# Who issues the second filter's two loads of a head: SyncE or ScalarE

## The reference, cut to what matters

```python
# 64 heads, head_dim 8; k = v = context, q = layernorm(x)
kv = einsum('bhil,bhjl->bijhl', k, v)
y = irfft(rfft(kv, 2L) * rfft(ssm_kernel, 2L))[..., :L]      # causal convolution along l, one filter per head
out = y + kv * D
x = x + tanh(g0) * einsum('bijhl,bhil->bjhl', out, q)
x = x + tanh(g1) * mixture_of_experts(layernorm(x))          # one shared expert, 7 routed, top 2, capacity 1170
```

## Time and profile before

| | |
|---|---|
| median of 3 runs | 4374.21 us (4369.9 to 4388.32) |
| profiled execution | 4357.41 us, span 4355.6 us |
| TensorE busy | 4130.0 us, 95% |
| VectorE, ScalarE, GpSimd busy | 60%, 44%, 23% |
| queue of SyncE (q1, hardware) | 413.89 MB, 31.6% of 16 DMA engines |
| queue of GpSimd (q0, software) | 218.41 MB, 26.7% |

### The profile page before, as it was taken

The page is one execution under the profiler, slowest core; times in us unless marked ns, Lnnn a source line. Parts: engine busy times, 40 slices in busy tenths (PEclk is TensorE's granted clock), DMA queues, the critical chain, the costliest instruction groups (busy, mean ns, idle before and its releaser), DMA issues.

```text
span 4355.6 us, 71272 instructions
## 1 busy us (share of the span) xinstructions
PE 4130.0 (95%) x25930; PEld 3766.7 (86%) x25930; DVE 2608.2 (60%) x2980; ACT 1898.5 (44%) x2451; POOL 997.7 (23%) x1200
## 2 busy tenths in 40 slices
PE   6999999999999999996899999999999999999997
PEld 6899999999999999996688888888888988988986
DVE  6899999999999999996434441222323332333331
ACT  6777777777777777774211111111112211121120
POOL 1232322232322332331000014451001211211111
PEclk9999999999999999998899999999999999999999
DMA  7878888878888888886532333423433443344332
GB/s 167 207 192 217 204 220 198 214 196 218 198 217 196 217 197 213 198 218 160 72 116 72 102 89 106 116 83 93 120 108 97 92 102 97 82 111 97 78 96 49
DMA packets 280375, 634.14 MB, mean 146 GB/s; under 512 B 45840, under 2 KB 111866, under 8 KB 280246
## 3 DMA queue, kind: packets, MB, share of 16 engines
q1 hardware_dynamic: 218582, 413.89, 31.6%
q0 software_dynamic: 61664, 218.41, 26.7%
HBM read 311.03 MB, written 170.16 MB: 110 GB/s over the span
## 4 chain that ended last, share of the span: by engine, by line
PE 48%; DMA 2%; DVE 1%; issue 1%; ACT 0%; SPq 0%; POOL 0%; DVEq 0%; POOLq 0%; ACTq 0%
PE moe_ps L1644 11%; PE moe_ps L1645 11%; PE moe_ps L1646 11%; PE moe_ps L1662 5%; PE moe_ps L1663 5%; PE moe_ps L1664 5%; PE moe_psT L1633 1%; DMA out<-moe_y,moe_add_i 1%; DVE moe_zl L1542 1%; DMA moe_y<-out 0%; ACT moe_zh L1314 0%; DMA out<-moe_y 0%; DVE moe_hid L1555 0%; DVE moe_y L1569 0%; DMA moe_zin<-zT_d 0%
## 5 line engine op out<-in xcount | busy, mean ns | idle before, releaser
L1644 PE MATMUL moe_ps<-moe_zh,moe_w1h 128*128 128x512 f32 (+2 forms) x2368 | 861.7, 364 | 36.9 <-DVE moe_zl L1542 22.9
L1645 PE MATMUL moe_ps<-moe_zl,moe_w1h 128*128 128x512 f32 (+2 forms) x2368 | 859.3, 363 | 0.0
L1646 PE MATMUL moe_ps<-moe_zh,moe_w1l 128*128 128x512 f32 (+2 forms) x2368 | 857.4, 362 | 0.0
L690 PE MATMUL att_psY<-att_kv_hi,att_tz_hi 128*128 128x288 f32 x2560 | 767.3, 300 | 40.2 <-DMA att_kv_lo<-att_kv 39.9
L692 PE MATMUL att_psY<-att_kv_hi,att_tz_lo 128*128 128x288 f32 x2560 | 756.0, 295 | 0.0
L691 PE MATMUL att_psY<-att_kv_lo,att_tz_hi 128*128 128x288 f32 x2560 | 755.6, 295 | 0.0
L1555 DVE TENSOR_TENSOR moe_hid<-moe_ps,moe_act_s 128x512 f32<-128x512 f32 (+2 forms) x148 | 91.6, 619 | 893.5 <-PE moe_ps L1646 869.5
L1644 PEld LDWEIGHTS moe_ps<-moe_zh,moe_w1h 128*128 128x128 f32 x2368 | 446.6, 189 | 89.8 <-issue 38.3
L690 PEld LDWEIGHTS att_psY<-att_kv_hi,att_tz_hi 128*128 128x128 f32 x2560 | 482.6, 189 | 41.2 <-issue 40.5
L1646 PEld LDWEIGHTS moe_ps<-moe_zh,moe_w1l 128*128 128x128 f32 x2368 | 447.9, 189 | 51.5
L1645 PEld LDWEIGHTS moe_ps<-moe_zl,moe_w1h 128*128 128x128 f32 x2368 | 447.2, 189 | 51.1 <-issue 0.2
(11 more groups left out here) (188 smaller groups left out, 7911.6 us busy)
## 6 DMA issues: line engine op xcount, KB each, us to landing
att_kv_lo<-att_kv POOLq DMA_DIRECT2D x128, 1152.0 KB, 13.4
att_kT<-in_cT SPq DMA_DIRECT2D x64, 512.0 KB, 12.8
att_xn<-in_x SPq DMA_DIRECT2D x64, 512.0 KB, 5.8
out<-att_x SPq DMA_DIRECT2D x64, 512.0 KB, 4.8
z_d<-att_z SPq DMA_DIRECT2D x64, 512.0 KB, 8.4
zT_d<-att_zT SPq DMA_DIRECT2D x64, 512.0 KB, 15.1
moe_zin<-zT_d SPq DMA_DIRECT2D x64, 512.0 KB, 5.0
moe_y<-out SPq DMA_DIRECT2D x128, 256.0 KB, 4.0
```

What stands on the lines that cost most here:

```text
L690: nc.tensor.matmul(acc, w_hi[:, cols], x_hi, start=start, stop=False, skip_group_check=True)
L1644: nc.tensor.matmul(acc, w1h[:, c, cols], zh[:, c, 0:w], start=(c == 0), stop=False)
L1645: nc.tensor.matmul(acc, w1h[:, c, cols], zl[:, c, 0:w], start=False, stop=False)
L1646: last = nc.tensor.matmul(acc, w1l[:, c, cols], zh[:, c, 0:w], start=False, stop=(c == C - 1))
```

## The change

`load_sums` moves word for word from SyncE's program to ScalarE's. SyncE issued it first in each head's step. ScalarE issues the load for head 0 ahead of all its own work and that for head h + 1 as the last thing in step h, behind `conv_out(h, 7)`. The wait (`y_done` at 8 times the head's number) is the same, and so are buffers, sizes and the semaphore `sz_in`. ScalarE issued no DMA before, so these two are alone in a queue of their own.

```diff
@@ SyncE
-            def load_sums(h):
-                wait(sp, y_done, NT * h)
-                sp.dma_start(sz_hi[:, :].bitcast(F32), s_hi[h]).then_inc(sz_in, 16)
-                sp.dma_start(sz_lo[:, :].bitcast(F32), s_lo[h]).then_inc(sz_in, 16)
-
             def step(h, u, ahead, back, back2):
-                load_sums(h)
                 if ahead:
                     load_filter(h + 1, 1 - u)
@@ ScalarE
+            def load_sums(h):
+                wait(act, y_done, NT * h)
+                act.dma_start(sz_hi[:, :].bitcast(F32), s_hi[h]).then_inc(sz_in, 16)
+                act.dma_start(sz_lo[:, :].bitcast(F32), s_lo[h]).then_inc(sz_in, 16)
+
+            load_sums(0)
             keys(0)
             keys_on(0)
...
                 conv_out(h, 7)
+                if ahead:
+                    load_sums(h + 1)
```

## The result

The changed kernel takes 4442.42 us (median of 4 runs, 4436.7 to 4447.28), the one before 4372.06 beside it: ratio 1.0164, 95% interval 1.0135 to 1.0193. It is 70 us slower. The profiled execution has a span of 4445.5 us.

A forecast was written before the change was run, and what follows sets the result against it. TensorE was taken to bound the convolution stage, its idle time being convolution 4's wait for `sz_lo`. Landings 0.4 us later in 60 heads add 24 us to 4374, ScalarE's issues nothing: 4398, said as 4400 us, range 4325 to 4485.

The forecast's parts named there:

- What bounds the kernel: Convolution stage: TensorE sets the pace; its one idle stretch, 1.53 us a head, is convolution 4 waiting for `sz_lo`.
- 60 us at the very most: Ceiling on the gain at convolution 4: `kv_lo` holds TensorE until 1014.3, so only 1.0 us in 60 heads can go.
- (a): Issue time of the second filter's loads on ScalarE: as early as before or half a microsecond later, taken as no difference.
- (b): DMA engines: three queues take turns, `kv_lo` lands 0.9 to 1.8 us later, together with `sz_lo`; convolution 4 0.4 us later.
- the term of 0.4 us a head: Convolution 4 starts at 1015.65, the middle of two cases, 0.4 us later than before, in 60 heads.
- The upper end I had, 0.87: Top of the forecast's case for convolution 4: start between 1015.3 and 1016.2, so 0 to 52 us more in all.
- (c): ScalarE's two issues cost it 2.4 us (bounds 0.8 to 5.3), delaying y_0 for convolution 2, hidden by convolution 4's wait: nothing.
- Nothing of these is on the path: SyncE, freed of 2.5 us a head, issues `tz`, the keys and zT earlier; counted as no effect.
- likeliest case: Convolution 4 starts at 1015.3 to 1016.2, 0 to 52 us more: 4374 to 4426 us, 40%.
- 1: Rival, faster: the third queue draws `sz` in early and `kv_lo` decides at 1014.3; down to 4314 us, 26%.
- 2: Rival, slower: issues cost ScalarE 5.3 us, y_0 is late and convolution 2 starts 3.8 us late; 130 us, 4505 us, 18%.
- 3: Rival, nothing moves: both arrivals at convolution 4 come again at 1015.2, or in another order; 4374 us within 10, 16%.

The follow-up runs named there:

- e3: The kernel before, with the z store issued behind the loads of the second and first filters instead of ahead: 4273.61 us, ratio 0.9775.
- e1: The changed kernel, with SyncE waiting until the second filter has landed before issuing the keys and then the first filter: 4347.44 us, ratio 0.9941.
- e9: The changed kernel, with the keys issued where SyncE issued the first filter, and the first filter only after the second has landed: 4374.47 us, ratio 1.0037.
- e2: The kernel before, with ScalarE kept busy about 2.3 us by six small copies behind the eviction of y_7: 4349.75 us, ratio 0.9940.
- e8: The kernel of e3 plus the six small ScalarE copies of e2: 4316.08 us, ratio 0.9885.
- e7: The kernel before, all on SyncE's queue, issuing the keys and then the first filter only after the second filter has landed: 4333.75 us, ratio 0.9922.
- e6: The changed kernel, with only `sz_hi` issued by ScalarE and `sz_lo` first in SyncE's step: 4311.84 us, ratio 0.9873.
- e4: The changed kernel, with the z store issued behind the first filter's loads as in e3: 4350.78 us, ratio 0.9954.

## Why the prediction was right or wrong

- **What bounds the kernel.** Right in the place. Too narrow in "60 us at the very most": I held `kv_lo` at 1014.3. That head's 13.6 us is the upper end; with the median of the second halves, 13.1, it lands at 1013.8, when TensorE is ready, and all of the wait could go. And it moves with the same queues, 11.4 us in e3 against 13.5 before (both halves), and e3 won 2.25%, 98 us.
- **(a) The time of issue.** Right in most heads: 0.22 us after the eviction's start, before 0.14. In the 13 heads above it is 0.93 before it: the sequencer issues at 1171.92, while the eviction that stands ahead in program order starts at 1172.86, behind other activations.
- **(b) What goes ahead on the DMA engines.** This is the step that failed: the term of 0.4 us a head, which measured 1.34. One to one to one is right (82, 82 and 81 packets in 3 us), and so is that `kv_lo` comes later: 0.9 us on the mean of the second halves (13.1 to 14.0), of the 0.9 to 1.8 forecast. I let the three queues start together, so that `sz` would have its 16 turns inside those of `kv_lo` and both would come at one time. In 12 of heads 6 to 57 it is like that or better for `sz`, and `kv_lo` is 1.4 us later on the median and decides. In most it isn't: ScalarE's queue starts 4 to 5 us after the issue, when `kv_lo` has had a good part of its turns against the z store alone. `kv_lo` is then only 0.7 us later, and `sz_lo` is left to share with the first filter what remains and lands 2.2 us after `kv_lo`, before 1.4. The upper end I had, 0.87, is passed too. e1 and e9 show the sharing by taking it away and dosing it; why the queue starts late is open.
- **(c) ScalarE.** The price was right in most heads, 0.36 + 2.05 us, taken 2.4; in the 13 with the early issue it is near the lower bound, 0.34 + 0.39. The consumer that is late first was missed: not convolution 2 for y_0, with 1.54 us to spare, but the transposes of z for zT, behind y_0 on ScalarE, with 0.7. So there is a wait of 1.5 us that the prediction doesn't name. That the wait at convolution 4 covers it was right; e2 shows it, e8 what it costs uncovered.
- **"Nothing of these is on the path".** Wrong. When they are issued is on the path: in the changed kernel the earlier first filter is what `sz_lo` shares with, and e7, which only issues the keys and the first filter later, wins 0.8%.
- **The sum.** 60 x 0.4 = 24 us against 70. The time is inside the range given, 4325 to 4485, and outside the likeliest case's, 4374 to 4426.
- **The rivals.** 1 did not come; its direction shows in e6. 2 did not come: ScalarE's second issue takes 2.0 us, as SyncE's did, though both engines issue at once. 3 did not come. The rule that a sequencer waits for the generator's lock (the Trainium skill, "Perfetto Trace Analysis", DMA Instruction — HWDGE) isn't borne out as a doubling: the issues of 1043.38 and 1043.42 start together and end together, after 2.06 and 2.05 us. That several issuing engines bring no more than issue time (the Trainium skill, "DMA: Bandwidth & Descriptors", Issuing engines are not separate DMA queues) agrees in that nothing was won by the third queue as such, but it leaves out who goes first: the changed kernel issues `sz_lo` at the same point of most heads as before (0.66 and 0.64 us after the eviction of y_7 starts), and it lands 1.3 us later. In e6, which won 1.3%, a part can be issue time, 0.45 us a head.

## What to carry to other kernels

A transfer moved to a queue of its own need not overtake: here it did in 12 of 52 heads, and what it overtook (`kv_lo`) was then waited for. Otherwise it takes turns with whatever the other queues hold from its start on, and a FIFO in which it stood ahead of the rest may have been its best place. List what stands ahead and what will stand beside it, per engine, before moving it, look at more than one head for when its queue starts, and look first for a store that nobody waits for and that can go behind. An engine's late work costs nothing under a longer wait and its full price once that wait is repaired, so it is worth reading off every consumer behind it, not only the next.

## What the runs showed of the hardware that was not expected

- A transfer issued on either hardware queue some 1.7 us after GpSimd's, with no transfer of its queue moving, sent its first packet only 4 to 5 us after its issue (e3 and e4, and ScalarE's in the changed kernel). The gap to GpSimd's issue varies within the trace of the changed kernel: at 1.7 us (36 heads) the first packet comes 4.1 to 5.0 us after ScalarE's issue, at 1.3 us (3 heads) after 2.9 to 3.0, at 0.8 to 0.95 us (13 heads) after 1.0 to 1.4. At 0.8 us it is ahead of GpSimd's own first packet, which then comes 3.2 to 3.4 us after GpSimd's issue instead of 1.8. The z store, issued 0.6 us after GpSimd's, moves 1.6 us after its issue. So it goes with the gap; by what mechanism is open, and no run set the gap.
- The second of two issues in a row takes 2.0 us on ScalarE as on SyncE beside GpSimd's transfer, also when ScalarE's queue holds nothing but the first. Without the z store ahead it is shorter, 1.33 us in e4; in the 13 heads with the early issue, before GpSimd's packets move, and at the very start, before GpSimd's first transfer, it is 0.39.
- ScalarE's sequencer issues a transfer while activations ahead of it in program order have not started: 0.94 us ahead in the head shown (1171.92 against 1172.86), where its semaphore count was there already.
